# All of a graph layer's row gathers put on GpSimd, with double-buffered sums

## The reference

```python
msg = relu(x[src] + edge_attr @ We + be)
aggr = segment_sum(msg, dst, num_segments=N)
h = (1.0 + eps) * x + aggr
h = relu(h @ W1 + b1) @ W2 + b2
mu, var = mean(h, axis=0), var(h, axis=0)
h = (h - mu) * rsqrt(var + BN_EPS) * gamma + beta
out = layernorm(x + (relu(h) + x), axis=-1)
```

## Time and profile before

| | |
|---|---|
| median of 3 executions | 1582.13 us |
| span of the profiled execution | 2684.1 us |
| TensorE, its weight loads | 70%, 51% of the span |
| VectorE, ScalarE, GpSimd | 37%, 31%, 43% |
| mean granted TensorE clock | 0.809 |

### The profile page before, as it was taken

The page is one execution under the profiler, slowest core; times in us unless marked ns, Lnnn a source line. Parts: engine busy times, 40 slices in busy tenths (PEclk is TensorE's granted clock), DMA queues, the critical chain, the costliest instruction groups (busy, mean ns, idle before and its releaser), DMA issues.

```text
span 2684.1 us, 58837 instructions
## 1 busy us (share of the span) xinstructions
PE 1871.5 (70%) x23395; PEld 1369.8 (51%) x23395; DVE 991.5 (37%) x3361; ACT 841.5 (31%) x1954; POOL 1154.5 (43%) x1193
## 2 busy tenths in 40 slices
PE   1776777776777777677767767767767776766776
PEld 0455555555555555555555555555555555555554
DVE  6433333333333333333333333333333333333335
ACT  3232323232332333232323323323223322322335
POOL 6444444444444444444444444434434444444421
PEclk9877788787887787788888778878778778887888
DMA  8222222232222222222222222222222222222221
GB/s 231 62 59 65 62 59 68 59 71 66 63 63 61 61 62 64 61 66 59 67 61 61 65 61 63 65 58 65 64 58 67 61 62 63 63 65 62 62 86 50
DMA packets 148455, 180.61 MB, mean 67 GB/s; under 512 B 41677, under 2 KB 128932, under 8 KB 147924
## 3 DMA queue, kind: packets, MB, share of 16 engines
q1 hardware_dynamic: 102489, 89.62, 14.0%
q0 software_dynamic: 37728, 77.31, 11.5%
q10 hardware_dynamic: 7963, 9.90, 1.2%
HBM read 170.09 MB, written 6.63 MB: 66 GB/s over the span
## 4 chain that ended last, share of the span: by engine, by line
PE 66%; issue 20%; another core or an unknown queue 8%; ACT 2%; DVE 1%; ACTq 0%; DVEq 0%
PE ps L1330 23%; PE ps L1315 15%; PE ps L1255 12%; PE ps L1269 11%; PE ps L1296 1%; PE ps L1276 1%; PE ps L1299 1%; ACT xg L694 1%; PE ps L1287 1%; PE ps L1384 1%; ACT slotS L680 0%; PE ps L1288 0%; PE ps L1394 0%; DVE lnst L1197 0%
## 5 line engine op out<-in xcount | busy, mean ns | idle before, releaser
L574 POOL DMA_INDIRECT xg<-xb,idxb x1145 | 1106.6, 966 | 1423.9 <-DVE msg L937 1068.8
L1330 PE MATMUL ps<-iota_all 128*128 128x128 bf16 x4032 | 377.8, 247 | 425.7 <-issue 291.3
L688 ACT ACTIVATE iota_all<-ps 128x384 bf16<-128x384 f32 x896 | 408.5, 489 | 775.6 <-remote 567.8
L1330 PEld LDWEIGHTS ps<-iota_all 128*128 128x128 bf16 x4032 | 290.1, 111 | 515.6 <-issue 511.5
L1022 DVE TENSOR_TENSOR accT<-accT,ps 128x64 f32 x390 | 86.5, 222 | 1138.4 <-remote 992.8
L1255 PE MATMUL ps<-we,ea 64*128 64x128 f32 x3126 | 344.2, 367 | 45.7 <-issue 45.3
L1330 PE MATMUL ps<-iota_all,hot_all 128*128 128x128 bf16 x4032 | 301.1, 229 | 102.6 <-issue 98.8
L937 DVE TENSOR_TENSOR msg<-ps,xg 128x512 f32<-128x512 f32 x390 | 262.0, 686 | 238.9 <-PE ps L1255 233.2
L1330 PEld LDWEIGHTS ps<-iota_all,hot_all 128*128 128x128 bf16 x4032 | 247.2, 102 | 172.4 <-issue 145.0
L1255 PEld LDWEIGHTS ps<-we,ea 64*128 64x128 f32 x3126 | 288.0, 261 | 80.7 <-issue 72.2
L1269 PE MATMUL ps<-msg,hot 128*64 128x128 f32 x3120 | 300.9, 352 | 6.2 <-issue 4.5
(11 more groups left out here) (135 smaller groups left out, 1113.8 us busy)
## 6 DMA issues: line engine op xcount, KB each, us to landing
ea<-in_eat SPq DMA_DIRECT2D x156, 320.0 KB
lowB<-lowD SPq DMA_DIRECT2D x128, 224.0 KB
xg<-xb,idxb POOLq DMA_INDIRECT x1145
accT<-in_xt ACTq DMA_DIRECT2D x1, 3125.0 KB
x<-in_xt ACTq DMA_DIRECT2D x1, 3125.0 KB
iota_all<-in_x ACTq DMA_DIRECT2D x1, 3080.0 KB
out<-iota_all SPq DMA_DIRECT2D x5, 512.0 KB
xb<-iota_all SPq DMA_DIRECT2D x3, 784.0 KB, 6.2
```

Source lines behind the costliest of these rows:

```text
L574: pool.indirect_dma_start(out=xg[0:rows, slot, j, :], out_offset=None, in_=of, in_offset=bass.IndirectOffsetOnAxis(ap=index, axis=0)).then ...
L688: act.activation(rows3[:, t, :, :].rearrange("p a h -> p (a h)"), ps_rows(k * NTILE + t), ACT.Copy)\
L1330: last = pe.matmul(found[:, e, :], sel2[set_of(k)][:, t, e * P:(e + 1) * P], rows3[:, t, a, :], start=(t == 0 and e == 0 and a == 0), stop ...
```

## The change

TensorE's gather goes with all that serves it: the split of x into `x3`, the ranking, the selection matrices, `pick`, `join`, `take`, the DMAs of `lowD` and `lowB`, the load of all of src. GpSimd gathers four tiles of each group. The indices are loaded into `idx_all` in three pieces at the start instead of through six small buffers. The blocks of x have 128 rows instead of 112, and x transposed has a buffer of its own, from which accT is made, so it isn't loaded a second time.

The linear sums and the sums by dst get two sets of banks each, winS two and msg and hot four buffers (TURN = 4). `window` runs two pairs after its `linear`, `turn` and `add_window` three (LAG = 3). The early chunks come one per pair in the last 12 pairs. One flag's inputs are computed at pairs 8 and 9, and the flags are read after the last pair. The last tiles' sums take the same way through winS and a transpose as all others.

```diff
-    RING = ROUND // 2
-    TURN = 3
+    RING = 15
+    TURN = 4
...
-        def ps_lin(half, j):
-            return ps[:, j // 2, (2 * half + j % 2) * HID:(2 * half + j % 2 + 1) * HID]
+        def ps_lin(m, half, j):
+            return ps[:, m % 2 * 2 + j // 2, (2 * half + j % 2) * HID:(2 * half + j % 2 + 1) * HID]
...
-        ps_win = ps[:, 2, 0:HID]
-        ps_turned = ps[:, 2, HID:2 * HID]
-        ps_end = ps[:, 3, 0:WIN]
+        def ps_win(m):
+            return ps[:, 4 + m % 2, 0:HID]
+
+        def ps_turned(m):
+            return ps[:, 4 + m % 2, HID:2 * HID]
...
+            for g in range(LOOPED):
+                h, at = divmod(g * GROUP, TILES)
...
+                if g == UNBIASED:
+                    for q in range(NQ):
+                        pool.wait_ge(s_xb[q], stores(q))
+                if g >= RING:
+                    wait_apart(pool, s_pre, g - RING + 1)
+                for j in range(GROUP):
+                    gather(g % RING, j, P, idx_all[:, h, at + j:at + j + 1], s_xg[g % RING], x if g < UNBIASED else xb)
...
+            for p in range(PAIRS):
+                if p >= 2:
+                    keep_sums(p - 2)
...
+                clip(p, 0)
+                clip(p, 1)
...
+            for q in range(NQ):
+                lift(q)
+            for p in range(PAIRS):
+                one_hot(p)
+                add_x(p, 0)
+                add_x(p, 1)
+                if p >= LAG:
+                    add_window(p - LAG)
...
+            for p in range(PAIRS):
+                if p >= 2:
+                    pe.wait_ge(s_pre, 2 * (p - 1))
+                for half in range(2):
+                    linear(p, half, ALL)
+                if p >= 2:
+                    window(p - 2)
+                if p >= LAG:
+                    turn(p - LAG)
...
+                for c in range(EARLY):
+                    if p == CLOSE + c:
...
+                        pe.wait_ge(s_acc, DONE[c])
+                        first_product(c, 0)
+                        if c:
+                            second_product(c - 1, 0)
+            pe.wait_ge(s_pre, 2 * (PAIRS - 1))
+            linear(PAIRS, 0, LAST)
+            second_product(EARLY - 1, 0)
+            window(PAIRS - 2)
+            turn(PAIRS - 3)
+            window(PAIRS - 1)
+            turn(PAIRS - 2)
+            window(PAIRS)
+            turn(PAIRS - 1)
+            turn(PAIRS)
+            general, redo = flags(pe)
```

More of the change, by code:

```diff
@@ L169, in gine_layer_kernel @@
         b1s, b2s, gms, bts, eps1 = (par[:, j:j + 1] for j in range(5))
[L171 to L192, removed]
+        winS = sb("winS", [P, 2, HID])
         bnst = sb("bnst", [HID, len(CHUNKS), 6])
@@ L1244, in _ @@
             pe.wait_ge(s_tr, 5)
-            pe.wait_ge(s_srcf, 1)
-            pe.transpose(ps[:, 3 + TBLK // 4, TBLK % 4 * P:TBLK % 4 * P + TREST], src_f[0:TREST, TBLK, :], ident[0:TREST, 0:TREST])
-            for b in range(TBLK):
-                last = pe.transpose(ps[:, 3 + b // 4, b % 4 * P:(b % 4 + 1) * P], src_f[:, b, :], ident[:, :])
-            last.then_inc(s_srcT, 1)
-            pe.wait_ge(s_we, 16 * 6)
-            def linear(h, s, half, tiles):
+            pe.wait_ge(s_we, 16 * 6)
@@ L1253, in linear @@
+            ALL = [(j, P) for j in (0, 2, 1, 3)]
+            def linear(m, half, tiles):
+                h, s = divmod(2 * m + half, SPAN)
+                if s == 0:
+                    pe.wait_ge(s_ea[h % PARTS], (h // PARTS + 1) * 32)
                 for j, r in tiles:
                     rows, at = slice(j // 2 * EDIM, (j // 2 + 1) * EDIM), j % 2 * P
-                    last = pe.matmul(ps_lin(half, j)[0:r, :], ea[h][rows, s, at:at + r], we2[rows, :], start=True, stop=True)
+                    last = pe.matmul(ps_lin(m, half, j)[0:r, :], ea[h % PARTS][rows, s, at:at + r], we2[rows, :],
+                                     start=True, stop=True)
@@ L1256, in linear @@
                 last.then_inc(s_lin, 1)
-            ALL = [(j, P) for j in (0, 2, 1, 3)]
-            def window(q, pair):
-                pe.wait_ge(s_msg, 2 * pair + 2)
-                pe.wait_ge(s_hot, pair + 1)
-                if not isinstance(pair, int) or pair:
-                    pe.wait_ge(s_winS, pair)
-                    pe.wait_ge(s_acc, 2 * pair)
-                for j in range(GROUP):
-                    for half in range(2):
-                        last = pe.matmul(ps_win[half * WIN:(half + 1) * WIN, :], hot[:, q % TURN, half * GROUP + j, :],
-                                         msg[:, q % TURN, half * GROUP + j, :], start=(j == 0), stop=(j == GROUP - 1))
-                last.then_inc(s_win, 1)
@@ new lines, in window @@
+            def window(m):
+                pe.wait_ge(s_msg, 2 * m + 2)
+                pe.wait_ge(s_hot, m + 1)
+                if m >= 2:
+                    pe.wait_ge(s_winS, m - 1)
+                    pe.wait_ge(s_acc, 2 * (m - 1))
+                if m < PAIRS:
+                    for j in range(GROUP):
+                        for half in range(2):
+                            last = pe.matmul(ps_win(m)[half * WIN:(half + 1) * WIN, :], hot[:, m % TURN, half * GROUP + j, :],
+                                             msg[:, m % TURN, half * GROUP + j, :], start=(j == 0), stop=(j == GROUP - 1))
+                else:
+                    for j, r in LAST:
+                        last = pe.matmul(ps_win(m)[0:WIN, :], hot[0:r, m % TURN, j, :], msg[0:r, m % TURN, j, :],
+                                         start=(j == 0), stop=(j == LASTT))
+                last.then_inc(s_win, 1)
@@ L1380, in first_product, with turn @@
+            def turn(m):
+                pe.wait_ge(s_winS, m + 1)
+                pe.transpose(ps_turned(m), winS[:, m % 2, :], ident[:, :]).then_inc(s_turned, 1)
             def first_product(c, z):
```

843 lines of the change are left out of this document (177 added, 666 removed).

## The result

The changed kernel takes 2060.53 us (median of four executions, 2060.11 to 2065.83) where the kernel before took 1582.34 beside it: 1.3025 times as long, 95% interval 1.2999 to 1.305. The forecast was 2035, its range 1975 to 2095. The profiled execution of after is the longest of its four, 5 us over the median; only this one has a trace, so what the 5 us are isn't known.

A forecast was written before the change was run, and what follows sets the result against it. GpSimd and TensorE were taken as nearly even before, GpSimd's gathers as the bound after: 1954.1 for start and gathers + 4.2 prologue + 28 one-hots + 44 tail = 2030, with 5 carried 2035 us; range 1975 to 2095.

The forecast's parts named there:

- nearly even: Kernel before: bills of 1562 us for GpSimd and 1567 for TensorE, so time alone doesn't say which binds.
- The gathers: GpSimd's loop: 1563 gathers in one queue, a straight sum at 1.248 us each, 1954.1 with the 3.45 before the first.
- upper bound of 1.29: Kernel before: a gather, with its gap and the 20 us missing from GpSimd's bill, can't have cost more than 1.29 us.
- VectorE beside a gather: Gathers slowed by the loop's 195 one-hots: 0 to 57 us, the middle 28 taken, 0.145 each.
- Prologue: Start of the kernel: VectorE's lifts and work on dst add 4.2 us to gathers, the same as before.
- wait for xb: Prologue: GpSimd's wait for xb falls from 8.4 us to 0, since 40 gathers come first; upper bound 8.4.
- The end: After the last gather: landing 2.3, sums through winS and transpose 4.7, flags 1, then 35.7; 44 us in all.
- Two sets, LAG, TURN: Loop buffering and later addition: cost nothing, gain nothing, as other engines need at most 8.4 us a pair against 9.98.
- Around the span: Time that may lie outside the profiled span or be waits for TensorE: 5 us carried of 0 to 20.
- A: Rival: each of 195 one-hots locks GpSimd out for its whole 0.68 us, 133 instead of 28, 2140 us; chance 0.06.
- B: Rival: the 0.30 us gap between gathers comes from recording; step 0.944, 1555 us, faster by 1.7%; chance 0.04.
- C: Rival: only part of the gap between gathers is real; step 0.961 to 1.20, 1582 to 1955 us; chance 0.08.

The follow-up runs named there:

- second profile: The kernel before, unchanged, profiled and timed once more: span 1582.1 us, time 1585.98 us, 1.0002 of its other executions.
- experiment 5: Kernel before with 240 GpSimd gathers left out: 1479.26 us; with 2688 join matmuls left out: 1586.75 us; with both left out: 1329.79 us.
- experiment 1: Changed kernel with one gather left out in every second group from group 15 on, 188 in all: 1821.94 us, 238.6 less than after.
- experiment 2: Changed kernel with one buffer each for linear sums, window sums and winS instead of two: 2056.84 us, 1.299 of before.
- Experiment 4: Changed kernel with the two flags read at pair 11 instead of after the last pair: 2059.55 us, 1.0 less than after.
- experiment 6: Changed kernel with one gather of a group's four from group 15 on: 642.33 us with two sets of sums, 1198.58 us with one.
- experiment 3: Changed kernel with the one-hot reading its column numbers from a PSUM bank, except in the last 14 pairs: 2014.45 us, 1.273 of before.

## Why the prediction was right, and where it was off

**What bounds before.** The prediction left it at "nearly even" from two bills, 1562 and 1567, and this step was wrong. GpSimd's bill was good to 20 us (1582.1 in the second profile; what lacked was mostly the disturbances by VectorE, 49 us of excess against the 30 that a busy 1142.9 held). TensorE's was 88 too high, 84 of it because 7.36 us a pair was taken from a stretch of the disturbed execution in which the clock was not full; experiment 5 shows 6.92 and a time of 1479. The forecast survived since it was made of gathers alone.

**The gathers.** 1563 x 1.248 = 1950.6 predicted, 1475.5 + 476.4 = 1951.9 in the profile; the slope of experiment 1 confirms it from the time. The upper bound of 1.29 held too. This term carries 95% of the span and, with 480 of 482 us, nearly all of the change.

**VectorE beside a gather.** 28 taken for the one-hots, 49.2 measured: the term that was most off, 21 of the 34 us by which the span of after exceeds 2030. That a gather pays only when it starts under a one-hot was right; what was missing is when it starts. A gather loses what the one-hot has still to run less 0.1, so starts spread evenly over the step of 1.25 would cost 0.58 x 0.58 / 2 / 1.25 = 0.135 each, 26 us in all, an estimate from these rows and close to the middle that was taken. They are not spread evenly: 158 gathers start during one of the 195 one-hots, where 0.68 / 1.25 makes 106, and 86 of them start 0.1 to 0.2 us after it began, at 0.42 each. Since each one-hot follows an addition that itself waits for a gather's landing, a fixed phase is what one would expect; that was argued from the order of the rows and not tried by itself. With one set of sums (experiment 2) the phase is another and the same 195 one-hots cost 38.5. The prediction's upper figure, 0.24 each from the lifts, makes 47 and is near the 0.252 measured, but nothing here shows that this is more than chance.

**Prologue.** Disturbances outside one-hots 55.5 - 49.2 = 6.3 for 4.2. The wait for xb, taken as 0, is 3.80 less a gap, 3.5: the stores of xb land at 61.5, not the 54.8 of the earlier trace rows; its bound of 8.4 held. What delayed them was not tried.

**The end.** 44 taken, 49.4 measured. The landing was right: the additions of the last tiles begin 2.2 us after the last gather (2.3 taken). From there to the end of the last addition to accT it is 6.8 where 4.7 stood: three pairs' sums follow each other through the copy, the transpose and the addition to accT, 3.2 us from one to the next. For the flags 1 was taken, with 0 to 3 as bounds, but 4.3 us pass between the last addition and the first product, where before has 0.05. Experiment 4 shows the pieces: about 1.5 us of loading the flags, part of it beside the last addition, and 3.8 of two branches, for which the prediction had no term. The rest is 36.1 for 35.7.

**Two sets, LAG, TURN.** "Cost nothing, gain nothing" is shown for the two sets by experiment 2: the ring of one set, 5.94 us a pair in experiment 6, is below the 9.98 of the gathers and within the 8.4 of the prediction. With few gathers the two sets are worth over 550 us. The four turns of msg and hot and the addition three pairs later were not changed in any run; that GpSimd waits for nothing in after says that they cost nothing, and whether they gain anything wasn't tried.

**Around the span.** 5 carried, 2.1 found.

Together: 2030.3 + 1.4 (gathers) + 21.2 (one-hots) + 2.1 (other disturbances) + 3.5 (xb) + 5.4 (end) = 2063.9, and 2063.7 is the span. Every term of size was measured above what the prediction took, so nothing of size cancelled; only what lies around the span came out smaller. The range's upper end, 2095, is itself a slip: 2087 with the bounds of landing and flags, 2.3 and 2 more, makes 2091.

**The rivals.** A, the lock for the whole length of the operation: 133 us for one-hots, measured 49.2, and none for the same 0.68 us once an input is in PSUM. The Trainium skill, page "SBUF — State Buffer", section "SBUF: two separate sides", counts among the operations of VectorE that shut GpSimd out, besides those in a two-port perf mode, the ones with two SBUF inputs against a GpSimd operation that reads SBUF, and says that whichever of the two starts first keeps the ports until it ends. So the prediction's 2140 was too much for this rule: by it a gather pays at most what the one-hot has still to run. The trace agrees that the order decides (a gather that starts during a one-hot loses the rest less 0.1, one that runs already loses nothing), and experiment 3 that it takes two inputs in SBUF. B and C needed a gap that isn't paid: experiment 1 has it at full price, and the time of after is 478 above before, where B had 27 below.

## What to carry to other kernels

Where one engine issues all of a kind of step, back to back, its time is count times start-to-start step, and what the other engines save or buffer is worth nothing until the count falls: ask first of any change what it does to that count. Code that leaves the loop still has to be priced at the end: a branch there cost 3.5 us. Before an engine is called the bound, see whether it waits, not how busy it is (90% here was slack, 74% the limit), and take no step time from a stretch whose clock differs from that of the timed executions. If VectorE works beside a queue of small DMAs that GpSimd issues, put an input of its long operations into PSUM. Letting them begin right behind the start of a gather should serve as well, by the gathers of after that were already running; that wasn't tried.

## What the runs showed of the hardware

- An indirect gather of 128 rows of 512 bytes keeps GpSimd about 0.944 us, and the next begins 0.305 later, in every kernel here where nothing else holds it; left out, one saves 1.269.
- A VectorE comparison of 0.68 us with both inputs in SBUF lengthens a gather that starts during it by what it has still to run less 0.1 us, up to 0.5, and one that was already running by nothing: 49.2 us in 2063.7. With one input in PSUM, at unchanged length of its own, it costs gathers 0.2 us, and the kernel takes 2014.45 instead of 2060.53.
- The same program had a profiled execution of 2684.1 us and another of 1582.1, with the same 23395 matmuls and the same step of gathers; the holes were on TensorE.
- TensorE's clock was 0.68 on average when a ring of dependences left it waiting in each pair, and 16 matmuls of 1.16 us then took 2.08.
- The same branch in TensorE's program, on the second flag, took 0.22 us in before and 3.0 to 3.5 in after and four of its variants; why is open.
